# Reordering the calls of five engine programs in a batch-pipelined decoder layer

## What is computed

```python
x = x + attn(layernorm(x))        # 16 heads of 32; windows of 128 keys, step 64; sigmoid weights over their sum;
                                  # one shared K and V head, rope, both rounded to an 8-bit grid; blend of windows; @ wo.T
x = x + wkv(w, u, layernorm(x), ctx)      # a scan over tokens: y = (A p + E v) / (A q + E)
h = silu(bit_linear(n, w_gate)) * bit_linear(n, w_up)     # n = layernorm(x); 512 -> 2048
x = x + bit_linear(rms_norm(h), w_down)                   # 2048 -> 512
# bit_linear: activations rounded to 8 bits by row, weights to -1, 0, 1 by their mean absolute value
```

## Time and profile before

| | us |
|---|---|
| runs: median (lowest to highest) of 3 | 1158.01 (1154.17 to 1159.81) |
| the profiled execution: time | 1150.44 |
| the profiled execution: span | 1149.1 |
| busy in the span: PE / DVE / ACT / POOL | 880.0 / 862.5 / 701.1 / 437.3 |
| granted TensorE clock, mean | 0.892 |

### The profile page before, as it was taken

How to read it: one execution, slowest core, us unless ns; L and a number is a source line. 1 busy time by engine, 2 the same in 40 slices (tenths; PEclk the granted TensorE clock), 3 DMA queues, 4 the chain that set the end, 5 groups by cost and what they waited for, 6 DMA issues and landing times.

```text
span 1149.1 us, 22079 instructions
## 1 busy us (share of the span) xinstructions
PE 880.0 (77%) x8388; PEld 539.3 (47%) x8388; DVE 862.5 (75%) x1630; ACT 701.1 (61%) x1179; POOL 437.3 (38%) x495
## 2 busy tenths in 40 slices
PE   6781464567788888888888879797979797977755
PEld 3341334344454545454555555555555555553322
DVE  4563557697878787878877888888878787877863
ACT  0113816257776858585858585858585858584633
POOL 2110111135344444444434444454535353535532
PEclk9896676679999898989898989899989898988978
DMA  8966416011323232333223141313131313122122
GB/s 301 305 210 241 159 37 200 5 39 56 78 77 65 90 66 89 60 95 59 89 57 88 52 103 48 100 50 105 52 102 49 106 47 108 47 67 58 43 56 64
DMA packets 148762, 106.93 MB, mean 93 GB/s; under 512 B 99792, under 2 KB 126128, under 8 KB 147504
## 3 DMA queue, kind: packets, MB, share of 16 engines
q1 hardware_dynamic: 142128, 101.48, 30.8%
q0 software_dynamic: 656, 2.63, 0.6%
q10 hardware_dynamic: 5872, 1.42, 0.6%
HBM read 65.65 MB, written 10.49 MB: 66 GB/s over the span
## 4 chain that ended last, share of the span: by engine, by line
PE 33%; ACT 22%; DVE 20%; issue 13%; DMA 7%; POOL 4%; SPq 1%; ACTq 0%; DVEq 0%; POOLq 0%
PE bank L582 8%; PE bank L523 7%; ACT arena L714 7%; PE bank L592 6%; PE bank L512 5%; ACT work L750 3%; ACT junk L766 2%; DVE wide L995 2%; DVE amax L1104 2%; ACT L714 2%; DVE rows L1039 2%; POOL work L1340 2%; DMA work<-in_wgT 2%; ACT L766 2%; DVE stats_wkv L1094 2%
## 5 line engine op out<-in xcount | busy, mean ns | idle before, releaser
L582 PE MATMUL bank<-w_up_gate,qT 128*128 128x512 bf16 x1024 | 239.7, 386 | 32.7 <-DMA qT<-q_tok 13.7
L1340 POOL TENSOR_TENSOR work<-junk,lnw 128x512 f32<-128x512 f32 x128 | 188.7, 1490 | 163.2 <-DVE junk L1138 148.0
L1323 POOL TENSOR_TENSOR sums<-sums,blend 128x448 f32<-128x448 f32 x64 | 73.3, 1167 | 273.3 <-ACT sums L726 266.0
L582 PEld LDWEIGHTS bank<-w_up_gate,qT 128*128 128x128 bf16 x1024 | 98.6, 99 | 149.7 <-ACT junk L766 17.2
L512 PE MATMUL bank<-wide,k_win 32*128 32x128 f32 x1536 | 78.6, 348 | 106.7 <-ACT arena L714 77.5
L493 PE MATMUL bank<-wide,wq_sb 128*128 128x256 f32 x512 | 118.0, 390 | 28.1 <-DVE rows L1039 28.1
L592 PE MATMUL bank<-w_down,work 128*128 128x512 bf16 x512 | 117.1, 383 | 22.3 <-DMA work<-work 11.3
L714 ACT ACTIVATE arena<-bank 128x384 f32<-128x384 f32 x256 | 104.9, 497 | 41.9 <-PE bank L512 41.8
L544 PE MATMUL bank<-wo_sb,wide 128*128 128x512 f32 x256 | 116.1, 608 | 15.5 <-DVE wide L1032 15.5
L512 PEld LDWEIGHTS bank<-wide,k_win 32*128 32x128 f32 x1536 | 64.0, 238 | 127.6 <-ACT arena L714 91.8
L493 PEld LDWEIGHTS bank<-wide,wq_sb 128*128 128x128 f32 x512 | 98.8, 195 | 53.3 <-issue 39.8
(11 more groups left out here) (150 smaller groups left out, 1598.1 us busy)
## 6 DMA issues: line engine op xcount, KB each, us to landing
rows<-in_x SPq DMA_DIRECT2D x24, 512.0 KB, 3.6
sums<-in_xT SPq DMA_DIRECT2D x16, 512.0 KB, 8.7
wide<-in_xT SPq DMA_DIRECT2D x16, 512.0 KB, 5.5
ctx_T<-in_ctxT SPq DMA_DIRECT2D x16, 512.0 KB, 4.1
wide<-wide SPq DMA_DIRECT2D x64, 128.0 KB, 2.1
out<-rows SPq DMA_DIRECT2D x32, 256.0 KB, 2.0
kv_b<-k_raw SPq DMA_DIRECT2D x16, 384.0 KB
wide<-in_x SPq DMA_DIRECT2D x8, 512.0 KB, 9.3
```

What stands on the lines that cost most here:

```text
L582: last = te.matmul(bank[4 + k % 4][:, :], qT[:, c, t * P:(t + 1) * P], w_up_gate[:, m, c, cols], start=c == 0, stop=c == NC - 1)
L1340: ge.tensor_tensor(hid_w[:, t, cols], hid[:, n % 2, :], lnw[:, cols], op=ALU.mult).then_inc(z_set.sem, 1)
```

## The change

No instruction is added or removed. In all five programs the same calls stand in another sequence.

- TensorE: before, down(g, 0, 0) stood ahead of scores(b, 1) and the three other quarters together behind nums(b, 2). Now down(g, 0, 1) stands between scores 1 and 2, down(g, 1, 0) behind scores 3 and down(g, 1, 1) behind nums(b, 0); dens(b, 3) and the nums are spread between.
- ScalarE: silu(f, 1, 1 to 3) and the squares behind them move from the next round's start to the end of the round; scale_hidden(f, 0) and scale_tokens follow there, set_keys comes behind them. Behind the sigmoids wkv_logs comes ahead of logs(b, 0), and the logs and inverses 2 and 3 form pairs. Silus and squares alternate one by one. The fourth GATE sum and the UP and DOWN sums move.
- VectorE: output(g, 0) and peak(f, 0) move to the end of the round, hidden_scale(g, 0) between the hidden pieces. In rounds 0 to 2 rope(0, 1) comes ahead of weight_mean(GATE), and the roundings are spread in other places.
- GpSimd: weight_total(UP) moves behind the fourth weigh_windows and hidden_rstd, first_state behind weigh_hidden(w, 0, 0).
- SP: the hidden transposes are interleaved with the query swaps, and store(g, 0) comes ahead of the load of the next queries.

```diff
@@ tensor_program
                 down(g, 0, 0)
             if do_b:
                 scores(b, 1)
+            if do_g:
+                down(g, 0, 1)
+            if do_b:
                 scores(b, 2)
                 scores(b, 3)
+            if do_g:
+                down(g, 1, 0)
+            if do_b:
                 dens(b, 0)
                 dens(b, 1)
                 dens(b, 2)
+                nums(b, 0)
+            if do_g:
+                down(g, 1, 1)
+            if do_b:
+                nums(b, 1)
                 dens(b, 3)
-                nums(b, 0)
-                nums(b, 1)
...
@@ scalar_program, end of a round
+            if do_f:
+                silu(f, 1, 0)
+                silu(f, 1, 1)
...
+                squares(f, 1, 0)
+                silu(f, 1, 2)
+                squares(f, 1, 1)
...
+                silu(f, 1, 3)
+                squares(f, 1, 2)
+                squares(f, 1, 3)
+                scale_hidden(f, 0)
+            if do_w:
+                scale_tokens(w)
+            if i == 0:
+                sum_weights(DOWN, 0)
...
@@ pool_program
                 weigh_windows(b, 0)
                 weigh_windows(b, 1)
+            if do_w:
+                outputs(w, 0)
+            if do_b:
                 weigh_windows(b, 2)
+                weigh_windows(b, 3)
+            if do_w:
+                outputs(w, 1)
+            if do_f:
+                hidden_rstd(f, 0)
             if i == 0:
                 weight_total(UP)
...
@@ sync_program
             if do_b:
                 turn_queries(b, 0)
+            if do_g:
+                turn_hidden(g, 0, 0)
+            if do_b:
+                turn_queries(b, 1)
+            if do_g:
+                turn_hidden(g, 0, 1)
...
```

194 lines of the change are left out of this document (87 added, 107 removed).

## The result

The changed kernel took **1105.37 us** (median of 4 executions, 1103.48 to 1107.51) against 1158.17 for the kernel before (4 executions, 1154.17 to 1159.81): ratio 0.955, 95% interval 0.952 to 0.958. The forecast was 1126.5 with a range of 1108 to 1146. It is faster, as forecast, but by 52.8 us and not by 31.5, and it lies outside the range. The profiled execution took 1107.51 (span 1106.2), the slowest of its four; that of before took 1150.44, less than all its timed ones. So the two traces differ by 42.9; of the ten more between the medians, 7.7 are in the other executions of before and 2.1 in those of the changed kernel.

What follows compares the result with a forecast made beforehand. No engine was full, so the order of waits set the time. Terms -13.5 (start), -1.5 (round 1), -14.3 (13 steady rounds), -2.2 (end) sum to -31.5: 1118.9 from the profiled 1150.44, 1126.5 on the median; range 1108 to 1146.

Steps and rivals of the forecast that it cites:

- Start: Round 0, up to the first attention normalise on VectorE: from 165.28 to about 151.8, -13.5 us; bounds -9 and -15.
- Round 1: A 1.90 us weight sum moves from between third log and last inverse to behind it: -1.5 us, bounds 0 and -2.
- Head of the round: Half the hidden scaling leaves the round's start, so first silu comes 0.4 us earlier; alternating silus and squares gives -0.1.
- Down quarters in the score groups: Each steady round: a quarter exceeds its 1.71 us gap, +0.1; last score group runs at full clock, -0.7.
- P: End of the last score-group sigmoids on ScalarE in a round; 25.45 us after the round's mark in the earlier trace.
- P to the next A: From the end of the sigmoids to the next attention normalise: GpSimd's chain to the peak search unmoved, 0 us.
- A: Mark of each round: start of attention normalise on VectorE; steady marks stood 58.01 us apart before.
- Round 2: The round after round 1, before the thirteen steady rounds: forecast to gain nothing.
- End: Last half-0 scaling and a scale computation leave the tail; last down projection starts near 1135.4, not 1137.63: -2.2 us.
- Rival 2: Steady rounds gain 1.8 us each, as the 0.73 denominator wait also goes: 1117 us; chance 0.14.
- Rival 4: Slower: hidden transpose issued before the second query swap delays rotation, scans and join; example 1168 us; chance 0.08.
- The marks 56.9 apart: Sign of the forecast: attention normalises of successive steady rounds 56.9 us apart; wrong if they stay 58 apart.

Runs made afterwards that it cites:

- the second pair: Kernel before and changed kernel, both unchanged, profiled again on one chip: changed 1103.98 us, ratio 0.955; 13 steady rounds 767.88 before, 729.85 changed.
- the try with the product first: Changed kernel with all score-group gaps filled, plus VectorE's hidden product (1,1) before its second quotient and TensorE's last gate product before two transposes: 1129.61 us, 0.977.

## Why the prediction was wrong

*Start* (-13.5): right; -12.4 and -14.5 in two pairs of profiles, -11.3 with the weights' calls alone. The chain (weigh, all-reduce 5.91 later, 7.26 behind it, just in time for the rstd) is as worked out. Round 1 (-1.5): right, -1.2.

*Head of the round* (-0.4 and -0.1): right; -0.42, and +0.34 when undone.

*Down quarters in the score groups* (+0.1 and -0.7): **the term of the sum that was mis-sized.** It priced the fall of the clock by the one instruction group in the earlier trace rows. The runs show -1.30. The same low stretch held the denominators, and the 0.73 of the earlier trace rows was their time at half speed. The forecast then let this 0.73 go by another edit (logarithms swapped) and gave it back by a third (inverses joined); the first did nothing at full clock (swapped back: +0.0), the third did cost what was said: the last weighing starts at P+12.49, in the run with only TensorE's gaps filled at P+11.82. The round of the earlier trace rows, from which the full-speed value came, was no round without a fall: its clock was 0.97, the fall came one group later, its wait for the denominator was still 0.69, and it took 57.24. Between 0.97 and 1.00 lay the part that was missed.

*P to the next A* (0, bounds 0 and -0.7): **the step that failed.** The start of the last weighing was right to 0.05; the durations behind it were taken as fixed. The reading under it, that GpSimd alone ends the wait for the peak search, was not in the earlier trace rows: the line at 812.63 shows no idle time, and VectorE's own work ran right up to it.

```profile
812.52 0.15 DVE L990 BATCH_NORM_AGGREGATE mv_wkv<-stats_wkv 128x2 f32<-128x6 f32 x1
```

Two chains end there together, VectorE's and GpSimd's, and the forecast priced one. GpSimd's durations fell by 1.10, and VectorE's part kept pace, for the order on VectorE changed: with the clock's and the head's parts taken off (58.00-1.30-0.34 = 56.36 against 55.71) 0.65 a round is left for all that stands behind P. The quotient put back costs 0.62, so VectorE's new order carries nearly all of it; in the kernel before the like moves alone were a loss, so it needs the others' orders. How much is collision and how much is VectorE's length was not taken apart, and that stays open. Round 2 (0): the same stretch; P is at A+31.5 in both, the peak search 2.3 earlier.

In a round at full clock the two misses are of one size: -0.70 for the clock, -0.65 behind P.

*What the sum left out*: the kinds of rounds. Of the first pair of profiles: 13 x -2.29 = -29.8; long rounds of before gone, 760.7-13x58.0 = -6.7; rounds of the changed kernel that fell or were longer, 733.6-13x55.71 = +9.4; together -27.1. In the second pair -29.8-13.9+5.6 = -38.1. The forecast knew that its execution lay 7.6 under the median, and shifted the result by it as if the change left that part alone; it took it away. So of the 21.1 us by which the median was missed, 11.4 are between the two traces (1107.51 against 1118.9) and the rest is this shift and the changed kernel's own spread.

*End* (-2.2): the mechanism is there and was paid back. Rounding of half 0 starts 0.69 after the end of the peak search instead of 2.90, but that search comes 1.15 later after its A, so the last down projection starts 0.92 earlier. TensorE then runs it at half clock for 5.2 us instead of 3.2:

```profile
1093.65 1.01 PE L593 MATMUL bank<-w_down,work 128*128 128x512 bf16 x2 [9.24 <-DMA work<-work]
1094.88 8.43 PE L593 MATMUL bank<-w_down,work 128*128 128x512 bf16 x29 [0.22 <-issue]
```

It ends 9.66 after its start instead of 8.61.

*The rivals.* Rival 2 (rounds gain 1.8, 1117) erred less, with luck: its 0.73 does come through with the gaps alone, by the clock and not by TensorE's shorter late stretch, but in the changed kernel the joined inverses take it back (P+12.49 again), and shorter durations make up for it. Rival 4 (slower through the swaps of queries): the second rotation, scans and join came earlier, not later (join at A+21.04 instead of 22.23). Of what was to show it: first mark and table load without a wait were as said, the last group at 0.95 in eight of thirteen rounds. The peak search starts when GpSimd's last weighing ends, but VectorE's work ends there too. The marks 56.9 apart were not as said: 56.4 in the mean, and that alone spoke of what was missed. The Trainium skill's page "GPSIMD Engine Reference", section "Instruction dispatch", has about 6 us for the first call to a freshly loaded kernel: 5.91 here agrees, and the way back took 7.26, as in the earlier trace rows.

## What to carry to other kernels

Price a fall of TensorE's clock by whole stretches: compare the mark-to-mark times of rounds that differ in their granted clock and in nothing else, and ask of each wait behind the fall whether it is one of order or of a half-speed producer. When an order changes beside a chain, its durations are not constants: two-input work of VectorE and GpSimd at the same time costs both, and a delay of 0.7 can become one of 2.4 when it brings such work together. A line without idle time in brackets shows no wait: look for a second chain that ends there. And an engine's new order is worth what the other engines' orders let through: alone, TensorE's was a loss of 1.1%, and its undoing a loss of 17% against the changed kernel.

## What the runs showed of the hardware

- GpSimd's two-input operation of 128x512 takes 1.28 in the median; one beside VectorE's values and rotation took 2.18. VectorE's refinement of 0.68 becomes 1.01, a blending of 0.36 becomes 1.25, two quotients of 1.28 become 2.36. The collisions move with every reordering; the sum of VectorE's busy time in a round shows them (47.9 or 46.9).
- TensorE's clock falls to 1.2 GHz behind two idle gaps of 1.71 ahead of score groups. With both filled, all score groups take 0.95, in each of the thirteen steady rounds of nine traces. With one left it falls in five to seven of thirteen rounds of the changed kernel, and in eight with TensorE's order alone; what decides in which was not found.
- Ahead of the queries TensorE idles 1.56 to 1.84 in most rounds, and they take 7.14. Behind an idle time of 1.91 to 2.11 they took 8.83 once in each of five traces, and 7.14 in others; behind 2.92 to 3.04, in the try with the product first, 8.75 to 8.83 in every round.
- After 9.24 us of idling the last down projection ran 5.2 us at 1.2 GHz, after 11.29 us of idling 3.2 us. The cause was not tried.
